# Decoder front end: first query piece, high parts and first query rows in another order

## Chip, cores and metric

The kernel runs on one core of a Trainium2 chip. The metric is the device time of one execution in microseconds (us), lower is better; where several runs are shown, their median counts.

## What is computed

A two layer decoder on x of shape (4, 256, 128) with a context of shape (4, 1601, 64). The change touches only the start: the end of the first sub-layer and the beginning of the second.

```
x = layernorm(x + L0_attn(x))             # distance attention, one head; all before about 38 us
x = layernorm(x + L0_xattn(x, ctx_512))   # 16 heads of 8
    # q, k, v   = heads(x @ Wq + bq), heads(x @ Wk + bk), heads(x @ Wv + bv)     "qs", "ks", values of x
    # qc        = heads(x @ Wcq + bcq)                                           "qc"
    # kc, vc    = heads(ctx @ Wck + bck), heads(ctx @ Wcv + bcv)                 "kc", values of the context
    # y = softmax(causal(q k^T / sqrt(8))) v + softmax(qc kc^T / sqrt(8)) vc ;  y @ Wp + bp
x = layernorm(x + L0_ffn(x))              # mixture of 8 experts, top 2
x = layernorm(x + L1_attn(x))             # gated complex recurrence
x = layernorm(x + L1_xattn(x, ctx, ctx))
x = layernorm(x + L1_ffn(x))
```

## The kernel before

**Split numbers.** The scores of the second sub-layer must be exact to float32 while the matmuls are bf16. So every projected query and key is split into three bf16 parts, high, middle and low, and a score is a matmul over 48 rows (6 products of parts by 8 channels of a head). The split is done in 22 pieces of at most 512 columns, numbered j. Pieces 0 to 3 are the context keys of batch 0 (piece 3 has 65 columns); 4, 5 and 6 are the qc, qs and ks projections of the first half of x (batches 0 and 1); 7, 8 and 9 the same of the second half; 10 to 21 are the context keys of the batches 1 to 3.

**One piece** passes through four engines. keys(j) on TensorE (PE, L592 for context, L595 for x) projects into one of two PSUM banks, j % 2. high(j) on ScalarE (ACT, L927 or L929) writes the bf16 high part. rest(j) on VectorE (DVE, L1054 or L1056) writes what is left over into rem, two buffers, j % 2. middle(j) on ACT (L934) rounds rem to the middle part. low_part(j) subtracts once more, on DVE for the pieces 4 to 6 (L1061), on GpSimd (POOL, L445) for all others.

The waits between them: keys(j) waits for rest(j-2), since that frees its bank. rest(j) waits for high(j), for middle(j-2) and for the low part of j-2, since these free its half of rem. middle(j) waits for rest(j). A piece of x waits, besides, for its half of the first layernorm's output (x_ready, L155).

**The layernorm** works per half c (512 columns): pe_ln(c), L129, centres by a matmul; act_ln(c), L139, squares; pe_ln2(c), L134, gives the variance; act_ln2(c), L144 and L150, takes its logarithm and exponential; dve_ln(c), L155, writes X.

**values(n)** projects values on PE (L612 context, L607 x) in blocks into two further PSUM banks, waiting for the copy of block n-2. The blocks 0 to 4 are context values of batch 0 and copied by DVE at L1074; 5 to 8 are values of x, two matmuls each, and copied with a bias at L1068.

**Order of work.** All engines run fixed lists in program order; nothing is rescheduled. Each list is written out by hand in one function per engine, and an engine stops at the first wait that isn't met. The lists for the pieces 4 to 9 are what the change edits, on PE, ACT and DVE.

**SyncE's queue (SP)** carries the parts to DRAM scratch and back, since a head's rows have to be brought together. split_out(kind, b), L361, writes the 6 part rows of one kind of one batch (three that are high parts of a query, then after a wait two middle, then after a wait one low). load_split(kind, m), L381, waits for all 6 at the first unit of a batch and reads them for unit m (4 heads) in two DMAs. load_context, L348, reads the context keys of a unit in two DMAs. An issue takes SP 0.4 to 0.6 us, whatever its transfer takes later. The semaphore slot_in of unit 0 counts the two context and two qc loads: the first score matmul needs those four and no others.

**The second sub-layer** then has 16 units (4 batches by 4 groups of heads) of 15 "halves". A half (half(h), L730) is two score matmuls of 128x512 whose maximum DVE takes (L1133). 22 halves run before the main loop; in that ramp the pieces 10 to 21 and the other context values are interleaved, one after nearly each half. The first half needs slot_in of unit 0, values(8) ahead of it on PE, and nothing else that is late. The main loop (from `for g in range(NU * NST)`) has 240 steps: scores again, transposed (L772), exponentials on ACT (L1009), outputs (L795), and one more half. Its first step waits for the row of maxima of unit 0, brought by four small DMAs (L389).

The lists that matter, PE, ACT and DVE:

```
PE : ... keys(3) pe_ln(1) values(0) pe_ln2(1) keys(4) keys(5) values(1) keys(6) values(2) ...
ACT: ... high(3) act_ln(1) middle(3) act_ln2(1) high(4) ; for j in 5..9: middle(j-1) high(j)
DVE: ... dve_ln(0) rest(3) values(0) dve_ln(1) rest(4) rest(5) low_part(4) values(1) rest(6) ...
```

Of the kernel before, what the change touches and what calls it, by code (L numbers as in the profile page):

```python
# [82 lines left out]
def decoder_program(nc, a, out):  # L83
    persistent = ExitStack()
    with persistent:
# [119 lines left out]
        with ExitStack() as st:  # L205
# [85 lines left out]
            def low_on_dve(j):  # L291

                return FIRST_X <= j < SECOND_X

            def lows(j):

                return (x_low if low_on_dve(j) else c_low), sum(low_on_dve(i) == low_on_dve(j) for i in range(j + 1))
# [42 lines left out]
            with nc.Block() as block:  # L340
                @block.sync
                def _(sp):
# [5 lines left out]
                            sp.dma_start(kc[s][head_rows(e)], kc_scr[b, row:row + HD].rearrange(  # L348
                                "c r j t -> (c r) (j t)")).then_inc(slot_in[s], 16)

                    def split_out(kind, b):

                        j = last_piece[groups.index((kind, b // 2))]
                        q = slice(b * TQ, (b + 1) * TQ)
                        rows = KPART if kind == "ks" else QPART
                        for part, ready in enumerate(((j_hi, j + 1), (j_mid, j + 1), lows(j))):
                            sp.wait_ge(*ready)
                            for r in range(6):
                                if rows[r] == part:
                                    src = xk[:, part, q] if kind == "ks" else xq[:, PART_AT[part], ("qc", "qs").index(kind), q]  # L360
                                    sp.dma_start(xs_scr[kind][b, :, r], src).then_inc(x_out[kind][b], 16)  # L361
# [10 lines left out]
                    def load_split(kind, m):  # L372

                        s, b, g = m % SLOTS, m // NG, m % NG
                        if g == 0:
                            sp.wait_ge(x_out[kind][b], 16 * 6)
                        for e in range(2):
                            row = 16 * g + HD * e
                            dst = ks[s][head_rows(e)] if kind == "ks" else qq[s][head_rows(e), ("qc", "qs").index(kind)]
                            src = xs_scr[kind][b, row:row + HD].rearrange("c r j t -> (c r) (j t)")  # L380
                            sp.dma_start(dst, src).then_inc(slot_in[s] if kind == "qc" else self_in[s], 16)  # L381
# [16 lines left out]
                    for j, c0, w in FIRST_SLABS:  # L398
                        for ready, part in (((j_hi, j + 1), hi), ((j_mid, j + 1), mid), (lows(j), low)):
                            sp.wait_ge(*ready)  # L400
                            for r in range(6):
                                if (hi, mid, low)[KPART[r]] is part:
                                    sp.dma_start(kc_scr[0, :, r, :, c0:c0 + w], part[:, 0, c0:c0 + w]).then_inc(first_out, 16)
                    sp.wait_ge(filled, 2 * SLOTS)
                    sp.wait_ge(*KEYS_OUT[0])
                    load_context(0)
                    split_out("qc", 0)
                    split_out("qs", 0)
                    load_split("qc", 0)
                    split_out("ks", 0)  # L410
                    load_split("qs", 0)
                    load_split("ks", 0)
# [170 lines left out]
                def _(pe):  # L583
# [13 lines left out]
                    def values(n):  # L597

                        if n >= 2:
                            wait_values_out(pe, n - 2)  # L600
                        b, t0, count = values_order[n] if values_order[n][0] != "x" else (values_order[n][1], None, 2)
                        w = H * VW
                        if t0 is not None:
                            pe.wait_ge(ld_ctx[b], 16)
                        for i in range(count):
                            if t0 is None:
                                last = pe.matmul(ps[:, 2 + n % 2, i * w:(i + 1) * w],  # L607
                                                 X[:, (2 * b + i) * 128:(2 * b + i + 1) * 128], wv_x, start=True, stop=True)
                            else:
                                t = t0 + i  # L610
                                k = 128 if t < NKT - 1 else KLAST
                                last = pe.matmul(ps[0:k, 2 + n % 2, i * w:(i + 1) * w],  # L612
                                                 ctx_t[:, b, t * 128:t * 128 + k], wcv, start=True, stop=True)
                        last.then_inc(v_ps, 1)
# [84 lines left out]
                    project(1)  # L699
                    keys(3)  # L700
                    pe_ln(1)
                    values(0)
                    pe_ln2(1)
                    keys(4)
                    keys(5)
                    values(1)
                    for i in range(3):
# [199 lines left out]
                def _(act):  # L907
# [24 lines left out]
                    def middle(j):  # L932
                        act.wait_ge(j_rem, j + 1)
                        act.activation(parts_of(j)[1], rem[:, j % 2, 0:pieces[j][2]], ACT.Copy).then_inc(j_mid, 1)  # L934
# [38 lines left out]
                    high(3)  # L973
                    act_ln(1)
                    middle(3)
                    act_ln2(1)
                    high(4)
                    for j in range(5, LATE_KEYS):
                        middle(j - 1)
                        high(j)  # L980
                    for h in range(HALVES + S1_LEAD):
                        if h == 0:
                            middle(LATE_KEYS - 1)
# [38 lines left out]
                def _(dve):  # L1022
# [84 lines left out]
                    residual(1)  # L1107
                    dve_ln(0)
                    rest(3)
                    values(0)  # L1110
                    dve_ln(1)
                    rest(4)
                    rest(5)
                    low_part(4)
                    values(1)
# [1422 lines left out]
```

## Time and profile before

| | us |
|---|---|
| median of 3 runs | 656.49 (656.16 to 658.83) |
| the profiled execution, its own time | 657.46 |
| its span from first to last instruction | 655.7 |
| PE busy | 605.3 (92%) |
| DVE busy | 518.6 (79%) |
| ACT busy | 448.8 (68%) |
| POOL busy | 217.6 (33%) |
| mean granted TensorE clock, share of full | 0.979 |

The time of an execution is its span and 1.76 us around it. A timeline row reads: start, duration, engine, line, operation, output <- inputs, count, and in brackets how long the engine had been idle and what ended that. PEld rows are weight loads beside the matmuls; SPq rows are the issue of a DMA, not its transfer.

### The profile page before, as it was taken

How to read it: one execution, taken by the hardware profiler on the slowest of the kernel's cores; microseconds unless marked ns; L12 is line 12 of the kernel's file. 1: busy time of each engine (PE TensorE's matmuls, PEld its weight loads, DVE VectorE, ACT ScalarE, POOL GpSimd, SP SyncE). 2: the span in 40 equal slices, each digit the busy share in tenths (PEclk: the TensorE clock that was granted, in tenths of full speed). 3: DMA queues.
4: the chain of work that ended last, by engine and by line, in shares of the span. 5: the costliest groups of instructions: out<-in, count | busy, mean ns of one | idle time of the engine just before them, and what ended most of it. 6: DMA issues, size and time to landing. Idle time of an engine off the chain costs nothing. (4 is left out here: it accounts for less than half of the span.)

```text
span 655.7 us, 13652 instructions
## 1 busy us (share of the span) xinstructions
PE 605.3 (92%) x5208; PEld 335.6 (51%) x5208; DVE 518.6 (79%) x710; ACT 448.8 (68%) x818; POOL 217.6 (33%) x296
## 2 busy tenths in 40 slices
PE   9989999999999999999999899999728799999995
PEld 5644544444444444444433468777214466567884
DVE  5369999999999999999963469889599468786532
ACT  3555589999999999999998445556681256666214
POOL 8214443335666576667665003010000000024000
PEclk9999999999999999999999979999959999999999
DMA  8357586566666444434320217893000100000000
GB/s 212 108 142 224 199 258 179 155 171 173 174 170 165 132 105 92 99 86 115 72 64 22 74 52 232 304 333 135 1 0 1 48 1 0 2 1 0 1 0 33
DMA packets 44895, 71.11 MB, mean 108 GB/s; under 512 B 13048, under 2 KB 32544, under 8 KB 44832
## 3 DMA queue, kind: packets, MB, share of 16 engines
q1 hardware_dynamic: 31840, 38.34, 22.3%
q0 software_dynamic: 12384, 29.66, 13.8%
q10 hardware_dynamic: 608, 2.25, 1.5%
q8 instruction: 41, 0.67, 0.4%
q14 instruction: 22, 0.18, 0.1%
HBM read 44.68 MB, written 24.80 MB: 106 GB/s over the span
## 5 line engine op out<-in xcount | busy, mean ns | idle before, releaser
L1009 ACT ACTIVATE prob<-ps 128x512 f32<-128x512 f32 (+2 forms) x480 | 250.9, 584 | 23.5 <-PE ps L772 15.4
L1133 DVE TENSOR_REDUCE pm<-ps 128x2 f32<-128x1024 f32 x192 | 224.1, 1209 | 5.7 <-PE ps L730 5.6
L795 PE MATMUL ps<-prob,vst 128*9 128x256 f32 (+1 forms) x1664 | 131.7, 381 | 3.2 <-ACT o_all L997 3.2
L772 PE MATMUL ps<-qq,kc 50*128 50x256 bf16 (+1 forms) x832 | 132.2, 273 | 0.6 <-DMA qq<-mrow 0.6
L730 PE MATMUL ps<-kc,qq 48*128 48x512 bf16 x384 | 117.3, 383 | 1.3 <-DVE pm L1133 1.2
L772 PEld LDWEIGHTS ps<-qq,kc 50*128 50x128 bf16 (+1 forms) x832 | 52.2, 95 | 96.2 <-ACT prob L1009 79.1
L795 PEld LDWEIGHTS ps<-prob,vst 128*9 128x9 f32 (+1 forms) x1664 | 27.7, 88 | 44.5 <-ACT prob L1009 28.2
L718 PE MATMUL ps<-masks_b 64*128 64x256 bf16 x256 | 38.0, 269 | 0.0
L730 PEld LDWEIGHTS ps<-kc,qq 48*128 48x128 bf16 x384 | 33.9, 93 | 6.9 <-DVE pm L1133 3.4
L1466 ACT ACTIVATE sg<-ps,exp_bias 128x512 f32<-128x512 f32 x32 | 22.0, 686 | 21.8 <-PE ps L1382 21.8
L535 POOL TENSOR_TENSOR o_all<-o_all,below 128x512 f32<-128x512 f32 x14 | 17.8, 1270 | 50.6 <-DMA below<-rden_scr 50.6
L1140 DVE TENSOR_REDUCE nm<-ps 128x4 f32<-128x512 f32 (+1 forms) x32 | 30.6, 957 | 2.0 <-PE ps L718 0.8
L1380 PE MATMUL ps<-x_high,up_high 128*128 128x512 f32 x64 | 26.7, 417 | 5.3 <-DMA exp_bias<-in_wexp 3.7
L545 POOL DMA_DIRECT2D R<-o_all x56 | 28.9, 522 | 4.1 <-POOL o_all L537 4.1
L2133 ACT ACTIVATE ctx_t<-ps,base 128x512 f32<-128x512 f32 x16 | 11.0, 688 | 27.8 <-PE ps L1863 27.8
L2075 ACT ACTIVATE ps<-shift 128x512 f32<-128x512 f32 (+1 forms) x28 | 15.7, 569 | 20.2 <-DVE shift L2328 14.1
L1566 DVE SCALAR_TENSOR_TENSOR hv<-ps,exp_bias,sg 128x512 f32<-128x512 f32 x32 | 24.0, 750 | 4.3 <-ACT sg L1466 4.2
L1471 ACT ACTIVATE hh_high<-whole 128x512 fp32r<-128x512 f32 x32 | 20.0, 626 | 10.4 <-DVE whole L1574 10.1
L1744 POOL TENSOR_TENSOR ctx<-ctx_t,ctx 128x512 fp32r<-128x512 f32 x4 | 5.2, 1290 | 65.5 <-DVE ctx L2340 65.5
L1382 PE MATMUL ps<-x_high,up_low 128*128 128x512 f32 x64 | 26.3, 411 | 0.0
L1381 PE MATMUL ps<-x_low,up_high 128*128 128x512 f32 x64 | 26.1, 408 | 0.0
L445 POOL TENSOR_TENSOR low<-rem,mid 128x512 bf16<-128x512 f32 (+1 forms) x16 | 14.6, 920 | 33.8 <-ACT mid L934 33.8
(369 smaller groups left out, 1262.6 us busy)
## 6 DMA issues: line engine op xcount, KB each, us to landing
kc<-kc_scr SPq DMA_DIRECT2D x32, 300.2 KB, 4.6
below<-rden_scr POOLq DMA_DIRECT2D x14, 256.0 KB, 6.0
comb_bc<-comb_scr SPq DMA_DIRECT2D x7, 512.0 KB, 6.1
ctx<-ctx_scr POOLq DMA_DIRECT2D x4, 801.0 KB, 7.0
raw<-in_wexp POOLq DMA_DIRECT2D x8, 384.0 KB, 6.4
exp_scr<-raw_high POOLq DMA_DIRECT2D x8, 384.0 KB, 4.7
exp_scr<-raw_low POOLq DMA_DIRECT2D x8, 384.0 KB, 6.0
kc_scr<-hi SPq DMA_DIRECT2D x6, 400.2 KB, 4.8
```

The source lines that it names most:

```text
L545: pool.dma_start(R[row:row + HD, b * TQ:(b + 1) * TQ], o_all[32 * hh:32 * hh + HD, n, 0:TQ]).then_inc(y_in[b], 16)
L718: done = pe.matmul(o, ident_b[rows, half, :], mask[rows, half, :].unsqueeze(1).to_broadcast([64, 2, 128]), start=False, stop=(half == 1), ...
L730: return pe.matmul(bank, qq[s][rows, 0, j, t * 128:(t + 1) * 128], kc[s][rows, j, c * 512:(c + 1) * 512], start=True, stop=True)
L772: last = pe.matmul(bank[0:p, j * TQ:(j + 1) * TQ], kc[s][rows, j, t * 128:t * 128 + p], qq[s][rows, 0, j, :], start=(j == 0), stop=True, s ...
L795: last = pe.matmul(o_ps[32 * hh:32 * hh + VW, kind * TQ + q0:(kind + 1) * TQ], value[:, hh * VW:(hh + 1) * VW], prob[0:k, (NST * n + t) % ...
L1009: act.activation(prob[0:p, g % P_RING, 2 * e:2 * e + 2, q0:TQ], s2[0:p, k % S2_RING, 0:2 * w].rearrange("p (i q) -> p i q", i=2), ACT.Exp, ...
L1133: dve.tensor_reduce(pm[:, m % 2, c, :, jt], banks, AX.X, ALU.max).then_inc(s1_read, 1)
L1140: dve.tensor_reduce(nm[:, :, 1, :].rearrange("p e (j t) -> p e j t", t=2)[:, :, :, t], banks[:, :, 0:2 * w].rearrange("p e (j n) -> p e j ...
L1380: pe.matmul(o, weight[0], x[0], start=start, stop=False, skip_group_check=True)
L1381: pe.matmul(o, weight[0], x[1], start=False, stop=False, skip_group_check=True)
L1382: return pe.matmul(o, weight[1], x[0], start=False, stop=True, skip_group_check=True)
L1566: dve.scalar_tensor_tensor(out=hv[:, k % 2, :], in0=ps[:, 2 + k % 2, :], scalar=exp_bias[s][:, NF + f:NF + f + 1], in1=sg[:, k % 2, :], op ...
```

## The change

Four edits, all in the lists of the front:

1. PE: keys(4) goes ahead of pe_ln2(1), and values(0) behind it.
2. ACT: high(4) goes ahead of act_ln2(1); and for the pieces 5 to 9, high(j) goes ahead of middle(j-1).
3. DVE: rest(4) goes ahead of values(0) and dve_ln(1).
4. SP: the six qc rows of batch 0 are written ahead of the context load of unit 0; and the qc load of unit 0 goes ahead of the middle and low rows of qs.

No operation is added or taken away. The compiled lists have the same operations, waits and shapes; the line numbers of the new kernel are one higher from L356 on.

```diff
@@ sync
-                    def split_out(kind, b):
+                    def split_out(kind, b, parts=range(3)):
...
-                        for part, ready in enumerate(((j_hi, j + 1), (j_mid, j + 1), lows(j))):
+                        for part, ready in [(i, ((j_hi, j + 1), (j_mid, j + 1), lows(j))[i]) for i in parts]:
...
                     sp.wait_ge(filled, 2 * SLOTS)
+                    split_out("qc", 0)
                     sp.wait_ge(*KEYS_OUT[0])
                     load_context(0)
-                    split_out("qc", 0)
-                    split_out("qs", 0)
+                    split_out("qs", 0, (0,))
                     load_split("qc", 0)
+                    split_out("qs", 0, (1, 2))
                     split_out("ks", 0)
@@ tensor
                     pe_ln(1)
+                    keys(4)
+                    pe_ln2(1)
                     values(0)
-                    pe_ln2(1)
-                    keys(4)
                     keys(5)
@@ scalar
                     middle(3)
+                    high(4)
                     act_ln2(1)
-                    high(4)
                     for j in range(5, LATE_KEYS):
+                        high(j)
                         middle(j - 1)
-                        high(j)
@@ vector
                     rest(3)
+                    rest(4)
                     values(0)
                     dve_ln(1)
-                    rest(4)
                     rest(5)
```

How the compiled lists move. TensorE from the projection of piece 3 to that of piece 5; L134 is the variance of the second half, L595 a piece of x, L612 the context values. Before:

```order
L592 MATMUL ps<-ctx_t,proj_w 128x65 [waits ld_ctx0,j_rem]
L129 MATMUL ps<-R,base 128x512 [waits g_r]
L612 MATMUL ps<-proj_w,ctx_t 128x144 [waits ld_ctx0]
L612 MATMUL ps<-proj_w,ctx_t 128x144 x2
L134 MATMUL ps<-qsq,base 128x512 [waits ln1_squared]
L595 MATMUL ps<-X,proj_w 128x512 [waits ln1_x,j_rem] x2
```

and now:

```order
L593 MATMUL ps<-ctx_t,proj_w 128x65 [waits ld_ctx0,j_rem]
L129 MATMUL ps<-R,base 128x512 [waits g_r]
L596 MATMUL ps<-X,proj_w 128x512 [waits ln1_x,j_rem]
L134 MATMUL ps<-qsq,base 128x512 [waits ln1_squared]
L613 MATMUL ps<-proj_w,ctx_t 128x144 [waits ld_ctx0]
L613 MATMUL ps<-proj_w,ctx_t 128x144 x2
L596 MATMUL ps<-X,proj_w 128x512 [waits ln1_x,j_rem]
```

Piece 4 now stands between the centring and the variance of the second half, and the values block comes after both.

ScalarE from the second half's squares to the middle part of piece 6; L929 is a high part, L934 a middle part, L144 and L150 the layernorm. Before:

```order
L139 ACTIVATE qsq<-ps 128x512 [waits ln1_centred]
L934 ACTIVATE mid<-rem 128x65 [waits j_rem]
L144 ACTIVATE ln_ln<-ps,base 128x512 [waits ln1_var]
L150 ACTIVATE ln_rstd<-ln_ln 128x512 [waits ln1_lnv]
L929 ACTIVATE xq<-ps,base 128x512 [waits j_ps]
L934 ACTIVATE xq<-rem 128x512 [waits j_rem]
L929 ACTIVATE xq<-ps,base 128x512 [waits j_ps]
L934 ACTIVATE xq<-rem 128x512 [waits j_rem]
L929 ACTIVATE xk<-ps,base 128x512 [waits j_ps]
L934 ACTIVATE xk<-rem 128x512 [waits j_rem]
```

and now:

```order
L139 ACTIVATE qsq<-ps 128x512 [waits ln1_centred]
L935 ACTIVATE mid<-rem 128x65 [waits j_rem]
L930 ACTIVATE xq<-ps,base 128x512 [waits j_ps]
L144 ACTIVATE ln_ln<-ps,base 128x512 [waits ln1_var]
L150 ACTIVATE ln_rstd<-ln_ln 128x512 [waits ln1_lnv]
L930 ACTIVATE xq<-ps,base 128x512 [waits j_ps]
L935 ACTIVATE xq<-rem 128x512 [waits j_rem]
L930 ACTIVATE xk<-ps,base 128x512 [waits j_ps]
L935 ACTIVATE xq<-rem 128x512 [waits j_rem]
```

The high part of a piece now comes before the middle part of the piece ahead of it, and that of piece 4 before the layernorm's last two steps.

SyncE's queue from the last context slab to the rows of ks, as one piece of the difference:

```order
 L403 DMA kc_scr<-low 64x2x577 [waits c_low]
-L348 DMA kc<-kc_scr 48x3202 [waits first_out,filled]
-L348 DMA kc<-kc_scr 48x3202
-L361 DMA qc_scr<-xq 64x2x256 [waits j_hi]
+L361 DMA qc_scr<-xq 64x2x256 [waits j_hi,filled]
 L361 DMA qc_scr<-xq 64x2x256 x2
 L361 DMA qc_scr<-xq 64x2x256 [waits j_mid]
 L361 DMA qc_scr<-xq 64x2x256
 L361 DMA qc_scr<-xq 64x2x256 [waits x_low]
-L361 DMA qs_scr<-xq 64x2x256 [waits j_hi]
-L361 DMA qs_scr<-xq 64x2x256 x2
+L348 DMA kc<-kc_scr 48x3202 [waits first_out]
+L348 DMA kc<-kc_scr 48x3202
+L361 DMA qs_scr<-xq 64x2x256 [waits j_hi]
+L361 DMA qs_scr<-xq 64x2x256 x2
+L381 DMA qq<-qc_scr 48x512 [waits qc_out0]
+L381 DMA qq<-qc_scr 48x512
 L361 DMA qs_scr<-xq 64x2x256 [waits j_mid]
 L361 DMA qs_scr<-xq 64x2x256
 L361 DMA qs_scr<-xq 64x2x256 [waits x_low]
-L381 DMA qq<-qc_scr 48x512 [waits qc_out0]
-L381 DMA qq<-qc_scr 48x512
```

The context load moved behind six writes, and the qc load ahead of three.

## Rows read from the trace of the kernel before

**Rows 1.** Busy time by stretch: engine busy us (instructions), PEclk, DMA share, GB/s
```profile
33.00:51.00 18.00, 14.61 (x60) 8.43 (x60) 11.28 (x21) 9.56 (x18) 3.88 (x5) 1.00 0.52 140
51.00:83.00 32.00, 30.14 (x177) 16.54 (x176) 29.99 (x38) 18.34 (x40) 14.21 (x19) 1.00 0.68 216
83.00:150.00 67.00, 66.35 (x903) 27.96 (x899) 64.73 (x72) 61.84 (x118) 25.54 (x36) 1.00 0.65 185
```

**Rows 2.** Timeline, the ramp's last reductions and the main loop's first matmul
```profile
78.09 12.52 DVE L1133 TENSOR_REDUCE pm<-ps 128x2 f32<-128x1024 f32 x11
...
82.58 0.27 PE L772 MATMUL ps<-qq,kc 50*128 50x256 bf16 x1 [0.58 <-DMA qq<-mrow]
```

**Rows 3.** Timeline, 33 to 51 us, the rows of the pieces 4 to 9
```profile
33.17 0.69 DVE L155 TENSOR_TENSOR X<-ps,ln_rstd 128x512 f32<-128x512 f32 x1 [0.20 <-ACT ln_rstd L150]
...
33.98 0.90 PE L612 MATMUL ps<-proj_w,ctx_t 128*128 128x144 f32 x6
...
34.83 1.13 PE L134 MATMUL ps<-qsq,base 128*128 128x512 f32 x2
...
36.00 0.69 ACT L144 ACTIVATE ln_ln<-ps,base 128x512 f32<-128x512 f32 x1 [1.07 <-PE ps L134]
...
36.42 0.60 SPq L403 DMA_DIRECT2D kc_scr<-low  x1
...
36.72 0.63 ACT L150 ACTIVATE ln_rstd<-ln_ln 128x512 f32<-128x512 f32 x1
...
37.25 0.67 ACT L929 ACTIVATE xq<-ps,base 128x512 bf16<-128x512 f32 x1
37.38 0.69 DVE L155 TENSOR_TENSOR X<-ps,ln_rstd 128x512 f32<-128x512 f32 x1 [1.85 <-ACT ln_rstd L150]
...
38.78 1.12 PE L595 MATMUL ps<-X,proj_w 128*128 128x512 f32 x2 [0.37 <-DVE rem L1056]
...
39.17 0.82 SPq L348 DMA_DIRECT2D kc<-kc_scr  x2
...
40.00 0.75 DVE L1056 SCALAR_TENSOR_TENSOR rem<-ps,base,xq 128x512 f32<-128x512 f32 x1 [1.27 <-ACT xq L929]
40.04 3.76 SPq L361 DMA_DIRECT2D qc_scr<-xq  x6
40.67 0.68 DVE L1061 TENSOR_TENSOR xq<-rem,xq 128x512 bf16<-128x512 f32 x1
40.78 0.63 ACT L934 ACTIVATE xq<-rem 128x512 bf16<-128x512 f32 x1 [0.82 <-DVE rem L1056]
...
41.32 0.67 ACT L929 ACTIVATE xk<-ps,base 128x512 bf16<-128x512 f32 x1
...
42.02 0.75 DVE L1056 SCALAR_TENSOR_TENSOR rem<-ps,base,xk 128x512 f32<-128x512 f32 x1 [0.16 <-ACT xk L929]
...
45.89 1.16 POOL L445 TENSOR_TENSOR xq<-rem,xq 128x512 bf16<-128x512 f32 x1 [10.57 <-ACT xq L934]
...
47.71 1.06 SPq L381 DMA_DIRECT2D qq<-qc_scr  x2
...
48.45 0.75 DVE L1056 SCALAR_TENSOR_TENSOR rem<-ps,base,xk 128x512 f32<-128x512 f32 x1 [1.06 <-ACT xk L929]
...
50.80 0.39 PE L730 MATMUL ps<-kc,qq 48*128 48x512 bf16 x2
```

**Rows 4.** Landing times of the DMAs of qq, of L361 and of L348
```profile
DMA to landing us min/median/max: 1.9/2.9/4.8
...
DMA to landing us min/median/max: 1.9/2.0/4.3
...
DMA to landing us min/median/max: 3.9/4.4/4.9
```

**Rows 5.** Busy time by stretch, columns as in rows 1, edges of a low clock
```profile
376.00:377.00 1.00, 1.00 (x3) 0.78 (x3) 0.69 (x1) 0.24 (x2) 0.00 (x0) 0.50 1.02 380
...
386.00:387.00 1.00, 1.00 (x10) 1.00 (x9) 0.10 (x1) 0.60 (x1) 0.00 (x0) 0.88 0.00 0
```

## Prediction, made before the changed kernel ran

> **What bounds the kernel now.** I read the busy times by stretch first [rows 1]. From 83 us on the main loop has TensorE busy 66.35 of 67.00 us; it is a fixed amount of work, and whatever makes it start earlier moves all behind it. In the ramp ahead of it, 51 to 83 us, VectorE has 29.99 of 32.00 and TensorE 30.14: full as well, and none of its work is changed. The loose stretch is 33 to 51 us, where TensorE has 14.61 of 18.00, VectorE 11.28 and ScalarE 9.56: a latency chain through four engines. The ramp hands over to the loop with VectorE's reductions back to back and TensorE waiting 0.58 us for the row of maxima of unit 0 [rows 2], both of which are timed by the ramp's start. So the question is how much sooner the first score matmul, now at 50.80 us, can start, and the kernel gains just that.
>
> The timeline of that stretch [rows 3] shows the cycle. rest(5) starts at 40.00, middle(5) follows at 40.78, high(6) only behind it at 41.32, rest(6) at 42.02: 2.02 us a piece, each step waiting for the one before. The bracket at 42.02 names high(6) as what VectorE waited for, the one at 48.45 names high(9), after 1.06 us idle. But high(j) doesn't depend on middle(j-1); only the list says so. The end of it: rest(9) at 48.45, four small values blocks with their copies, first score at 50.80, which is 2.35 us later.
>
> The other thing that the first score needs is the qc load of unit 0. It is issued at 47.71 over 1.06 us; such loads land after 1.9 to 4.8 us [rows 4]. With 2.0 the second, issued about 48.25, is there at 50.25: not the last wait, but within 0.55 us of it. So the three engines' edits alone could give only some 0.5 us, and SP's alone nothing; both are needed.
>
> **The sum, part by part.** Steps used, all from [rows 3]: a projection takes TensorE 1.12 us and a values block 0.90, and the next block can begin a little before the end (the variance at 34.83, 0.85 after the values block's start); I estimate 0.96 and 0.90 from start to start, and with the full 1.12 the four projections up to keys(7) would come out 0.6 later in all; what reads a projection starts 1.16 after it (the variance at 34.83 is read at 36.00); high to rest 0.70 (41.32 to 42.02); rest to middle 0.78 (40.00 to 40.78); one to the next on ScalarE 0.54 (40.78 to 41.32); middle to a low part 0.70 too; a rest holds VectorE 0.67 (40.00 to 40.67), a low part some 0.60, and I take the same for a copy.
>
> *Piece 4 ahead of the variance.* X of the first half is written at 33.17+0.69=33.86, and TensorE takes its next block at 33.98. keys(4) takes that slot instead of values(0). high(4) at 35.15 instead of 37.25, rest(4) at 35.85. The price: the variance starts at 34.94 or a little more instead of 34.83, since the squares were ready but TensorE is held 0.1 longer; the logarithm goes from 36.00 to about 36.14, dve_ln(1) from 37.38 to 37.52. I charge 0.14 us, and it falls on nobody: X of the second half is first read by keys(7), which comes at about 40.6. values(0) goes back to 35.95, copied at 36.9, ahead of dve_ln(1) on VectorE; its copy ends by 37.5, so it costs dve_ln(1) nothing more.
>
> *Pieces 5 and 6.* keys(5) stands behind values(0): 35.95+0.90=36.85. high(5) 38.00, rest(5) 38.70 (was 40.00), middle(4) 38.55, low_part(4) 39.35 (was 40.67). keys(6) follows values(1) at 38.71, high(6) 39.86, rest(6) 40.56 (was 42.02), middle(5) 40.42.
>
> *Piece 7 gives some of it back.* keys(7) follows values(2) at 40.57, high(7) 41.72. middle(6) now stands behind high(7): 42.27, and low_part(6) needs it: 42.97. VectorE's list has rest(7) behind low_part(6), so rest(7) starts at 43.57, 3.01 after rest(6). This is the cost of the swap on ScalarE: every middle part comes later against its own rest than it did. It is the narrowest point of my chain.
>
> *Pieces 8 and 9.* keys(8) at 42.43 isn't held by it, high(8) 43.58, rest(8) behind rest(7) and a copy at 44.84. keys(9) waits for rest(7), 43.57+0.78=44.35; high(9) 45.51, and rest(9) could start at 46.21. It also waits for the low part of piece 7, on POOL: middle(7) at 43.57+0.78=44.35, POOL at 45.05, 1.16 us long, 46.21. The two agree, so I take 46.25. Against 48.45 that is 2.20 us, and the first score is free to start at 46.25+2.35=48.60.
>
> *SP.* The last slab row is issued by 37.02. qc high rows: three at about 0.6, to 38.8 (6 in 3.76). Middle(4) ends 38.55+0.63=39.2: two rows to 40.4. Low_part(4) ends at 40.0: one row to 41.0. Context load 41.0 to 41.9 (39.17 before), landing by 4.9 at the latest: 46.8 or so. That is 1.8 us ahead of 48.60, so moving it later costs nothing. qs high rows to 43.7. The qc load waits for the last of the qc rows, issued about 40.4 and landing within 2.0 to 4.3: 44.7 at worst. Its two issues end between 44.8 and 45.8, against 48.77 before. What is pushed back: three qs rows by one load, and those feed the self scores, the last two of the unit's 15 halves; SP as a whole has nothing more to issue than before and starts 2 us sooner.
>
> How late does that load land? In the trace loads of qq took 1.9 to 4.8 [rows 4]. With 1.9 the second lands at about 46.7, with 4.8 at about 49.5, which would be 0.9 us after 48.60. The first is nearest to the load it replaces, alone in its stretch; but now the context load runs beside it until about 46. I take 3 us, 47.7: hidden, by 0.9. The Trainium skill ("DMA: Bandwidth & Descriptors", section "Issuing engines are not separate DMA queues") says that all transfers share the same 16 DMA engines and interleave, whoever issues them; by it alone the qc load would be slowed by the context load beside it, which speaks for the 4.8 and a gain of 1.3.
>
> **Sum:** 2.2 us, between 1.3 (load lands late, or the 0.6 of the projections and a little more) and 2.9 (each of the seven handovers behind keys(4) a tenth shorter than I took it). The profiled execution took 657.46, so by its own account 655.3; the median of the runs is 656.49, 0.97 lower, and the forecast is made against that: 654.3 us. That is 0.33%, and less than the 0.5% (3.3 us) that a measurement of this kernel can tell from no change.
>
> **Rivals.**
>
> *A, the gain is mostly lost before the first score: 655.5.* Either the load lands at its worst and rest(7) slips behind the later middle(6) by another half microsecond, or the handover at 82.58 has a price that I don't see, the four small DMAs of the maxima meeting other transfers. For it: the DMA share is already 0.68 in the ramp. Against it: SP is ahead of, not behind, its old times. Gain 0 to 1.2.
>
> *B, the clock falls once more: 659.7.* In this trace TensorE's granted clock drops from 2.4 to 1.2 GHz at 376 us, behind two short idle spells in the expert stage's start, and is back in the slice that begins at 386 [rows 5], 10.9 us in all. Everything after the front now runs 2.2 us sooner against whatever times that decision. Should such a fall come on another thin place on TensorE's path, it costs at most half its length, 5.4 us, and the sum is 656.49-2.2+5.4=659.7, slower than before by 0.49%; a longer one would pass 0.5%. It decides at a TensorE busy share that is near what made it fall at 376. Against it: work and gaps behind the front are the same. The Trainium skill ("TensorE: Matmul & The Clock Gate", Part 1) says that the monitor's phase isn't tied to a kernel's start, so that the same kernel can vary from run to run; by that rule the shift changes nothing in the median, which already samples it.
>
> *C, the fall at 376 doesn't come: 648.9.* The same mechanism the other way: at most half of the 10.9 us would be saved, 5.4: 656.49-2.2-5.4=648.9 at the lowest.
>
> *D, the change doesn't do what it says:* keys(4) not taking the slot at 33.98, because X's semaphore comes after TensorE has gone to wait elsewhere. TensorE's list has nothing in between, so it would just wait; it costs 0.1 to 0.2 us and the variance behind it as much. It is inside my range.
>
> **How the numbers follow.** Forecast with its bounds 0.76; A 0.13; B 0.05, of which 0.03 beyond 0.5%; C 0.04; left over 0.02. Faster by over 0.5% (below 653.2) needs C, or the upper end of the forecast with a lucky median: 0.04+0.04=0.08. Slower by over 0.5% (above 659.8): 0.03. Same: 0.89. The range goes from the upper bound of the gain, 656.49-2.9=653.6, widened to 652.9 for the spread of medians, to 656.6, which takes in A and a median as high as before's own.
>
> **What would show it.** The first score matmul (L731 there) at 48.6, within 0.6; rest(4) at about 35.9; rest(7) at 43.6, with VectorE having waited for ScalarE's middle part ahead of it; dve_ln(1) at 37.5; SP's qc load at 44 to 45; the first matmul of the main loop at 80.4; each later stage shifted by the same 2.2. I am wrong if the first score names the DMA of qq as what it waited for, if it starts at 48.6 but the loop doesn't start at 80.4, or if the stages behind 83 us have other lengths than before.

## The result, and the profile after

| | us |
|---|---|
| the change, median of 6 runs | 652.53 (651.38 to 653.23) |
| before, median of 6 runs | 657.14 (656.16 to 658.83) |
| ratio | 0.9938, 95% interval 0.9916 to 0.9959 |
| the change's profiled execution, its span | 652.77, 651.0 |

The change is faster by 0.6%, 4.1 us by the ratio. All 19 executions of the change in this study have a median of 652.5, all 104 of the kernel before one of 656.4: 3.9 us (3.2 to 4.5 by resampling them). I forecast 2.2. Single executions of either kernel lie over 4 to 9 us, so below every difference is read twice: as a time, and as a place in the profile.

The busy times by stretch of the change, which answer to [rows 1]:

```profile
31.00:49.00 18.00, 15.44 (x67) 9.20 (x66) 13.32 (x24) 11.46 (x20) 4.90 (x5) 1.00 0.55 140
49.00:81.00 32.00, 30.06 (x180) 16.62 (x181) 29.95 (x38) 19.14 (x42) 15.10 (x20) 1.00 0.71 225
81.00:148.00 67.00, 66.35 (x906) 28.16 (x902) 64.72 (x72) 61.76 (x119) 25.60 (x35) 1.00 0.63 181
```

Ramp and main loop are what they were (66.35 of 67.00 us on TensorE in both); only the stretch ahead is fuller. Its timeline answers to [rows 2] and [rows 3]; columns as there, line numbers one higher:

```profile
33.12 0.69 DVE L155 TENSOR_TENSOR X<-ps,ln_rstd 128x512 f32<-128x512 f32 x1 [0.20 <-ACT ln_rstd L150]
...
33.95 1.10 PE L596 MATMUL ps<-X,proj_w 128*128 128x512 f32 x2
...
34.89 1.02 PE L134 MATMUL ps<-qsq,base 128*128 128x512 f32 x2
...
35.75 0.90 PE L613 MATMUL ps<-proj_w,ctx_t 128*128 128x144 f32 x6
35.81 0.75 DVE L1057 SCALAR_TENSOR_TENSOR rem<-ps,base,xq 128x512 f32<-128x512 f32 x1 [1.87 <-ACT xq L930]
...
36.48 1.02 PE L596 MATMUL ps<-X,proj_w 128*128 128x512 f32 x2
...
37.33 0.69 DVE L155 TENSOR_TENSOR X<-ps,ln_rstd 128x512 f32<-128x512 f32 x1
37.34 0.90 PE L613 MATMUL ps<-proj_w,ctx_t 128*128 128x144 f32 x6
...
38.08 1.02 PE L596 MATMUL ps<-X,proj_w 128*128 128x512 f32 x2
...
39.67 1.02 PE L596 MATMUL ps<-X,proj_w 128*128 128x512 f32 x2
...
41.30 0.60 DVE L1075 COPY vst<-ps 128x432 f32<-128x432 f32 x1
41.31 0.62 ACT L935 ACTIVATE xk<-rem 128x512 bf16<-128x512 f32 x1
41.97 0.69 DVE L1062 TENSOR_TENSOR xk<-rem,xk 128x512 bf16<-128x512 f32 x1
...
42.57 0.75 DVE L1057 SCALAR_TENSOR_TENSOR rem<-ps,base,xq 128x512 f32<-128x512 f32 x1
...
43.84 1.06 SPq L381 DMA_DIRECT2D qq<-qc_scr  x2
44.06 1.17 POOL L446 TENSOR_TENSOR xq<-rem,xq 128x512 bf16<-128x512 f32 x1 [8.79 <-ACT xq L935]
...
45.36 0.75 DVE L1057 SCALAR_TENSOR_TENSOR rem<-ps,base,xk 128x512 f32<-128x512 f32 x1 [0.66 <-POOL xq L446]
...
46.53 1.25 PE L608 MATMUL ps<-proj_w,X 128*128 128x144 f32 x8 [1.01 <-DVE vss L1069]
...
47.80 0.39 PE L731 MATMUL ps<-kc,qq 48*128 48x512 bf16 x2
```

The first score is at 47.80 instead of 50.80, and 2.95 us of it are the change's, since the row at 33.12 ahead of it had come 0.05 sooner. The cycle is broken: the projections of the pieces 5, 6 and 7 start at 36.48, 38.08 and 39.67, 1.59 us apart. Before, those of the pieces 6 and 7 waited for a rest, at 38.78 [rows 3] and 2.03 us later:

```profile
40.81 1.12 PE L595 MATMUL ps<-X,proj_w 128*128 128x512 f32 x2 [0.16 <-DVE rem L1056]
```

The main loop's first matmul shows that all of it arrives:

```profile
79.67 0.27 PE L773 MATMUL ps<-qq,kc 50*128 50x256 bf16 x1 [0.66 <-DMA qq<-mrow]
```

79.67 against 82.58 is 2.91. The two profiled executions differ by 4.7 us of span, though. The other 1.7 come in the expert stage, where the clock differs:

```profile
371.00:372.00 1.00, 1.00 (x2) 0.00 (x0) 0.00 (x0) 0.00 (x0) 0.00 (x0) 0.58 0.94 272
...
374.00:375.00 1.00, 1.00 (x4) 0.77 (x4) 0.42 (x1) 0.55 (x1) 0.00 (x0) 0.72 0.96 310
...
378.00:379.00 1.00, 1.00 (x4) 0.81 (x3) 0.97 (x12) 0.99 (x2) 0.00 (x0) 0.50 0.00 0
...
381.00:382.00 1.00, 1.00 (x9) 1.00 (x9) 0.75 (x1) 0.06 (x1) 0.00 (x0) 0.80 0.00 0
```

In this execution TensorE ran at 1.2 GHz from 371 to 375 and from 378 to 382, 6.8 us in all; in that of before for 10.2 at one stretch (the clock column of [rows 5] has it at half from 376 to 386 and for the first quarter of the slice behind; the prediction has 10.9). Whether that belongs to the change was the question for the experiments.

### The profile page after: what moved, and what is told of

Read it like the earlier page. It is cut to its first block and busy times, and to the rows that moved or that the text cites. A ratio compares the mean times of both kernels' runs of the same rounds, so it can differ in the third digit from the quotient of the medians.

```text
span 651.0 us, 13652 instructions
## 1 busy us (share of the span) xinstructions
PE 602.3 (93%) x5208; PEld 333.6 (51%) x5208; DVE 518.1 (80%) x710; ACT 448.9 (69%) x818; POOL 216.9 (33%) x296
## 5 line engine op out<-in xcount | busy, mean ns | idle before, releaser
L796 PEld LDWEIGHTS ps<-prob,vst 128*9 128x9 f32 (+1 forms) x1664 | 27.7, 88 | 44.5 <-ACT prob L1010 28.2
```

The lines of the kernel that those rows point to most:

```text
L796: last = pe.matmul(o_ps[32 * hh:32 * hh + VW, kind * TQ + q0:(kind + 1) * TQ], value[:, hh * VW:(hh + 1) * VW], prob[0:k, (NST * n + t) % ...
```

## Experiments

Every row of this table is one profiled execution. X is the start of the first half's layernorm product (L155), which no edit touches; the next two columns are the distances from it to the first score and to the main loop's first matmul. "Clock" says whether the granted clock fell to half at 49 to 54 us, and "expert stage" is the time from the layernorm matmul at its start to the last of its residual sums. "Median" and number of executions belong to that kernel's own runs.

| kernel | X to first score | X to loop | clock | expert stage | median (n) |
|---|---|---|---|---|---|
| before | 17.63 | 49.41 | no fall | 88.59 | 656.4 (104, all) |
| before_again | 17.90 | 51.04 | falls | 85.57 | |
| before_look3 | 17.83 | 50.95 | falls | 86.89 | |
| before_look4 | 17.64 | 49.41 | no fall | 88.43 | |
| the change | 14.68 | 46.55 | no fall | 86.90 | 652.5 (19, all) |
| after_again | 14.64 | 46.49 | no fall | 85.87 | |
| after_look3 | 14.58 | 46.44 | no fall | 86.49 | |
| e1_sp_old | 16.79 | 50.01 | falls | 86.57 | 657.7 (12) |
| e2_sp_only | 18.29 | 51.26 | falls | 88.15 | 656.0 (12) |
| e3_no_piece4 | 15.64 | 47.79 | no fall | 88.05 | 654.1 (12) |
| e4_no_swap | 16.11 | 48.30 | no fall | 85.80 | 655.0 (12) |
| e5_rest7_first | 14.77 | 46.63 | no fall | 86.03 | 652.3 (12) |
| e6_before_filled | 17.63 | 49.58 | no fall | 88.00 | 655.4 (12) |
| e7_load_first | 14.12 | 46.12 | no fall | 85.24 | 652.3 (9) |

**e1_sp_old: the engines' edits without SP's.**

```diff
+                    sp.wait_ge(*KEYS_OUT[0])
+                    load_context(0)
                     split_out("qc", 0)
-                    sp.wait_ge(*KEYS_OUT[0])
-                    load_context(0)
-                    split_out("qs", 0, (0,))
+                    split_out("qs", 0)
                     load_split("qc", 0)
-                    split_out("qs", 0, (1, 2))
```

> The change with SP's list as it was before; the other three engines' lists as changed. My theory: the first score needs both the engines' edits and SP's. With the old list the context load goes at about 39.2, six qc and six qs writes follow without a gap, the qc load of unit 0 is issued at about 47.3 and lands about 2 us after its second half, so the first score matmul waits for the DMA of qq and starts at 49.6 to 50.0 (50.80 before, 47.80 in the change); the time is 0.8 to 1.2 us below before. Rival (the queue's order is worth nothing, since the load was hidden): first score at 47.8, gain as in the change.

```profile
47.20 1.06 SPq L381 DMA_DIRECT2D qq<-qc_scr  x2
...
49.87 0.39 PE L730 MATMUL ps<-kc,qq 48*128 48x512 bf16 x2 [2.15 <-issue]
50.20 2.08 PE L592 MATMUL ps<-ctx_t,proj_w 128*128 128x512 f32 x2
...
53.55 1.22 DVE L1133 TENSOR_REDUCE pm<-ps 128x2 f32<-128x1024 f32 x1
```

The place was right: load at 47.20, first score at 49.87, TensorE idle for 2.15 us ahead of it. ("issue" means that the profile shows no releaser; the second load went out at about 47.8 and the two landed after 1.9 to 2.1, so it is the load.) The time was wrong: 657.7, ratio 1.0029 (1.0006 to 1.0053), so slower than before and not 0.8 to 1.2 us faster. Behind the idle spell the clock fell:

```profile
50.00:51.00 1.00, 1.00 (x3) 0.50 (x2) 0.70 (x1) 0.00 (x0) 0.00 (x0) 0.60 0.43 119
```

The projection behind the score then takes 2.08 us instead of 1.13 (50.20), and the second reduction begins 3.25 us after the first (50.30 to 53.55); in the kernel before these are 2.24 apart. From first score to loop it took 33.22 us against 31.78 in the kernel before, 1.4 us given back, so the loop starts 0.6 later than in the executions of the kernel before without a fall. That doesn't explain the whole median: over its 12 executions the mean clock was 0.9781, against 0.9829 for the kernel before beside it, and one fall as at 50 us (3.4 us at half clock in 655) lowers it by 0.0026. So in others there were further or longer falls; where, no profile here shows. At equal mean clock (by the line in the last section) e1 is 1.0 us below before, 0.4 to 1.5 with 95%: the 0.8 to 1.2 that I had expected of the order, and the clock took more than that back.

**e2_sp_only: SP's list alone**, PE, ACT and DVE as before.

> Only SP's list as changed; the other engines as before. My theory: the qc load is issued at about 46.3 or sooner, but TensorE reaches the first score at 50.8 as before: within 0.2 us of before up to the end of the main loop (first loop matmul at 82.6). Rival (the load was the last wait before): first score up to 0.5 us sooner. For the second question, where 1.7 us beyond the front came from: if they hang on the shift of the later stages, this kernel shows none of it; if they vary from run to run, it may show some.

Load issued at 44.7, and the first score no sooner: 18.29 from X against 17.63, later by 0.66, in an execution whose clock fell just before 50 us: the values block ahead of the score took 1.91 us instead of 1.25. 656.0, ratio 1.0000 (0.9975 to 1.0025). No gain of SP's part alone is seen. With e1, which brings the first score 0.8 sooner, this settles that neither part gives the 3 us without the other.

**e3_no_piece4: the swap and SP's list, piece 4 where it was.**

```diff
-                    keys(4)
-                    pe_ln2(1)
                     values(0)
+                    pe_ln2(1)
+                    keys(4)
...
-                    high(4)
                     act_ln2(1)
+                    high(4)
...
-                    rest(4)
                     values(0)
                     dve_ln(1)
+                    rest(4)
```

> The change without piece 4 ahead of the second half's variance (PE, ACT and DVE lists of that place as before); the swap of high and middle for the pieces 5 to 9 and SP's list kept. My theory: the swap breaks the 2.0 us cycle by itself, and piece 4 early gives a head start that only partly lasts: high(4) at 37.3, first score at about 48.5, 0.7 later than in the change. Rival (piece 4 is the whole gain, the swap nothing): first score at 50.5 or later.

First score 15.64 from X: 2.0 sooner than before and 1.0 later than the change, where I had 0.7. Of the 1.0 TensorE waited the last 0.23 us, by the same reading as in e1 for the qc load, which went out at 44.7 here. Ratio 0.9963 (0.9942 to 0.9984).

**e4_no_swap: piece 4 early and SP's list, middle(j-1) ahead of high(j) as before.**

```diff
                     for j in range(5, LATE_KEYS):
-                        high(j)
                         middle(j - 1)
+                        high(j)
```

> The change without the swap of high(j) and middle(j-1) for the pieces 5 to 9; piece 4 early and SP's list kept. My theory: the old cycle of about 2.02 us a piece comes back, from rest(5) at about 38.6 instead of 40.00, so the first score is at about 49.4, 1.4 before the old kernel's and 1.6 after the change's. Rival (the swap only moves the wait to the later middle parts and gives nothing): first score at 47.8.

First score at 16.11 from X: 1.5 sooner than before, 1.5 later than the change. The cycle is back in its rows, 2.03 us from rest to rest, with the same waits as before:

```profile
38.38 0.75 DVE L1057 SCALAR_TENSOR_TENSOR rem<-ps,base,xq 128x512 f32<-128x512 f32 x1 [0.41 <-ACT xq L930]
...
39.17 0.63 ACT L935 ACTIVATE xq<-rem 128x512 bf16<-128x512 f32 x1 [0.82 <-DVE rem L1057]
39.71 0.67 ACT L930 ACTIVATE xk<-ps,base 128x512 bf16<-128x512 f32 x1
40.41 0.75 DVE L1057 SCALAR_TENSOR_TENSOR rem<-ps,base,xk 128x512 f32<-128x512 f32 x1 [0.16 <-ACT xk L930]
```

The time, 655.0 with a ratio of 0.9986 (0.9963 to 1.0008), is smaller in its gain than 1.5 us but its interval holds that. So of the 3.0 us at the first score piece 4 gives 1.0 on top of the swap and 1.5 without it, the swap 1.5 on top of piece 4 and 2.0 without it. At the loop's start e3 and e4 are only 1.6 and 1.1 sooner than before: 0.4 us of their gain are lost in the ramp, which happens to neither kernel of the first pair; why, no run here shows.

**before_again, after_again, before_look3, before_look4 and after_look3** are the two kernels unchanged.

> The kernel before, unchanged, for a second profile and for the mean granted clock of many runs beside the change's. Theory 1 (what the change gains beyond the 3.0 us of the first score comes from the clock, which falls in some executions at TensorE's idle spell ahead of the first score): some of its executions have the fall at about 50 us; its mean clock over the runs is below that of the change by 0.001 to 0.002. Theory 2 (the excess of the first comparison was luck in few runs): equal mean clock.

> The change, unchanged, in more runs. Theory 1: 4 to 4.6 us below before, of which 3.0 at equal clock (5.4 us of time go with 0.01 of mean clock in the runs so far) and the rest by a higher mean clock; no fall at 46 to 54 us in its profile. Theory 2: 3.0 us below before at the same mean clock.

> The kernel before once more, for its profile alone: does the clock fall at about 50 us? So far it did in one profile of two of this kernel, and in one of one with TensorE's list of before and SP's changed. Theory (the idle spells at 46 to 50 us leave it near the fall): in some profiles; where it falls, the first score starts at 51.0 or later after the same upstream times, and the main loop about 1.3 us later than where it doesn't.

> As the run above: a fourth profile of the kernel before. Fall at about 50 us or not, loop start at about 83.9 or 82.5.

> The change once more, for its profile alone. Theory: no fall at 46 to 54 us, as in both profiles so far, first score at 47.5 to 47.8, loop start at 79.4 to 79.7. Rival (the change has the same fall in other executions): a fall there and a loop start above 80.5.

Two places were missed in them: before_look3 has the fall and its first score at 50.77, not 51.0 or later, and the last profile of the change starts it at 47.39, below 47.5 (both had X earlier, at 32.94 and 32.81).

The kernel before runs in two ways at 50 us. The rows of before_again, with the fall:

```profile
50.00:51.00 1.00, 1.00 (x9) 0.72 (x7) 0.46 (x1) 0.00 (x0) 0.99 (x1) 0.67 0.31 88
52.00:53.00 1.00, 1.00 (x2) 0.01 (x1) 0.85 (x1) 0.00 (x0) 0.00 (x0) 0.50 0.38 106
53.00:54.00 1.00, 1.00 (x4) 0.17 (x3) 0.00 (x0) 0.38 (x1) 0.00 (x0) 0.62 0.32 84
```

and in before_look4, without:

```profile
50.00:51.00 1.00, 1.00 (x8) 0.63 (x7) 0.88 (x3) 0.00 (x0) 0.78 (x1) 1.00 0.43 120
51.00:52.00 1.00, 1.00 (x4) 0.19 (x3) 1.00 (x2) 0.04 (x1) 0.00 (x0) 1.00 0.28 76
```

What goes before it is TensorE's two spells of idling, which end at 47.34 and 49.51:

```profile
47.34 0.76 PE L607 MATMUL ps<-proj_w,X 128*128 128x144 f32 x4 [0.62 <-DVE vst L1074]
...
49.51 1.53 PE L607 MATMUL ps<-proj_w,X 128*128 128x144 f32 x8 [1.42 <-DVE vss L1068]
```

But before_look4, without a fall, has the same two:

```profile
47.12 0.76 PE L607 MATMUL ps<-proj_w,X 128*128 128x144 f32 x4 [0.62 <-DVE vst L1074]
...
49.30 1.25 PE L607 MATMUL ps<-proj_w,X 128*128 128x144 f32 x8 [1.42 <-DVE vss L1068]
```

The loop is 1.5 to 1.6 us later in the executions with the fall (50.95 and 51.04 from X, against 49.41 twice). It came in two of four profiles of the kernel before and in e2, which has the same TensorE list; e4 has the same two spells and no fall. It came in none of three of the change, whose last idle spell is 1.01 us. So the spells of 0.62 and 1.42 us were followed by a fall in three of six profiles; 0 of 3 against that can be chance, and that the spells cause it is argued, not shown.

A sum by this account would be 3.0 us of list order, and in about half of the executions 1.5 more, 3.7 on the mean; measured were 3.9 between the medians of all runs. The record doesn't bear the second term out. after_again gave 652.6 with a ratio of 0.9959 (0.9933 to 0.9985), and a mean clock over 12 runs of 0.9820, below the 0.9829 of before_again, against theory 1. Over all runs the mean clock of both kernels is the same to 0.001, and at equal mean clock the change is still 3.7 us below before (3.2 to 4.1 with 95%), not 3.0. And what the fall costs at the loop's start isn't seen in whole executions: the two profiled ones of the kernel before with the fall took 655.76 and 656.92 us, the two without it 657.46 and 658.68, and the clock was low for less time in the former (23.3 and 24.4 us in all, against 26.3 and 25.0). So 3.0 us are shown by place, and some 0.7 more were measured whose source is open. e3 shows how far such sums can be off: at equal mean clock it is 2.9 us below before, with a loop start only 1.6 sooner.

**The expert stage** varies in one and the same kernel: 85.57 to 88.59 in the executions of the kernel before, 85.87 to 86.90 in those of the change, 85.24 to 88.15 in the others, whose code there is the same. It goes with its own low clock: without any it took 85.2 to 86.0 us (e4, e5, e7), with 10.2 us of it 88.1 to 88.6 (before, e2, e3). The 1.7 us of the first pair of profiles are within that spread. Whether the earlier start shifts the odds there, three profiles against four can't tell. The table's loop distances are what the list order is shown to be worth.

**e6_before_filled: the kernel before with the idle spell filled.**

```diff
                     for i in range(4):
+                        if i == 2:
+                            pe.wait_ge(masks_cast, 1)
+                            still = masks_b[:].rearrange("p i h n -> p (i h n)")
+                            for _ in range(6):
+                                pe.matmul(ps[:, 7, :], still[:, 0:128], still[:, 0:512], start=True, stop=True)
                         values(5 + i)
```

> The kernel before with six matmuls of 128x512 (results unused) on TensorE between values(6) and values(7), where it otherwise waits 1.4 us ahead of the first score; nothing else moves. Theory 1: the first score stays at 50.8 (within 0.2), the fall of the clock at about 50 us goes away, the mean clock over the runs rises by 0.001 or more and the median falls by 0.5 to 1 us. Theory 2 (no such fall, or it costs nothing, since VectorE bounds the ramp): time and clock as before.

```profile
47.83 1.46 PE L716 MATMUL ps<-masks_b 128*128 128x512 bf16 x6
49.41 1.25 PE L607 MATMUL ps<-proj_w,X 128*128 128x144 f32 x8
50.59 0.39 PE L735 MATMUL ps<-kc,qq 48*128 48x512 bf16 x2
```

First score where it was (17.63), no fall in its one profile, which half of the profiles of the kernel before don't have either. 655.4 against 656.2 for the kernel before beside it, mean clock 0.9836 against 0.9827: the way of theory 1, but the ratio is 0.9996 (0.9970 to 1.0022), so inconclusive.

**e5_rest7_first: a better order on VectorE.**

```diff
                     values(2)
+                    rest(7)
                     low_part(6)
-                    for i in range(2):
-                        rest(7 + i)
-                        values(3 + i)
+                    rest(8)
+                    values(3)
+                    values(4)
                     rest(9)
```

> The change, and on DVE rest(7) ahead of low_part(6), rest(8) ahead of the copy values(3). It aims at the place where the swap on ScalarE cost something: in the change's profile rest(7) starts at 42.57 behind a low part that waited for the later middle(6), while high(7) is ready for it at 41.4. Theory: rest(7) at 41.9, keys(9) 0.7 sooner, middle(7) and POOL's low part of piece 7 0.6 to 0.7 sooner, rest(9) at 44.7, first score at 47.1 (47.80 in the change), the time 0.7 below the change's. Rival (POOL's low parts or ScalarE are the bound at that point): first score within 0.2 of 47.8.

```profile
41.65 0.74 DVE L1057 SCALAR_TENSOR_TENSOR rem<-ps,base,xq 128x512 f32<-128x512 f32 x1
...
43.67 1.05 SPq L381 DMA_DIRECT2D qq<-qc_scr  x2
...
44.71 0.75 DVE L1057 SCALAR_TENSOR_TENSOR rem<-ps,base,xk 128x512 f32<-128x512 f32 x1
...
45.88 1.25 PE L608 MATMUL ps<-proj_w,X 128*128 128x144 f32 x8 [0.20 <-DVE vss L1069]
...
47.71 0.39 PE L731 MATMUL ps<-kc,qq 48*128 48x512 bf16 x2 [0.58 <-issue]
```

rest(7) at 41.65 and rest(9) at 44.71 came as forecast (0.18 of that from an earlier X), and TensorE was done with its values at 47.13. It then idled 0.58 us: the qc load, second half out at about 44.3, takes 3.3 to 3.5 us beside the context load, so it lands at 47.6 or a little later. The 0.5 us won on the engines, counted from X, were lost at the load, a limit that I had not seen right behind the one removed. So the first score and the time were missed (47.71 and 652.3, not 47.1 and 0.7 below the change's 652.5); the place is the rival's, by another cause than the rival's.

**e7_load_first: the same, and the qc load ahead of all qs rows.**

```diff
-                    split_out("qs", 0, (0,))
                     load_split("qc", 0)
-                    split_out("qs", 0, (1, 2))
+                    split_out("qs", 0)
```

> The run with rest(7) first, and on SP the qc load of unit 0 ahead of all qs rows. In the run with rest(7) first the engines were ready sooner, but the first score waited for the qc load, issued at 43.67 and landed 3.3 us after its second half. Theory: the load goes out as soon as the qc rows have landed, at about 42.5, lands by 46.5, and the first score starts when TensorE reaches it, at 47.1; loop start at about 79.0; 0.6 us below the change. Rival (the load moves but lands late beside the context load, 4 us and more): first score at 47.5 or later.

```profile
41.08 1.05 SPq L348 DMA_DIRECT2D kc<-kc_scr  x2
42.41 0.77 SPq L381 DMA_DIRECT2D qq<-qc_scr  x2
43.22 3.76 SPq L361 DMA_DIRECT2D qs_scr<-xq  x6
...
46.25 1.25 PE L607 MATMUL ps<-proj_w,X 128*128 128x144 f32 x8 [0.20 <-DVE vss L1068]
...
47.43 0.39 PE L730 MATMUL ps<-kc,qq 48*128 48x512 bf16 x2
```

The load went out 1.3 us sooner, 0.3 us behind the context load's issue, and took 4.3 to 4.5 instead of 3.3 to 3.5: the rival's landing time, but the wait is gone. The first score came at 47.43, not 47.1, since X was 0.4 late here (33.31). From X the first score comes 0.5 and the loop 0.4 sooner than in the change. Its median, 652.3 (9 runs, ratio to before 0.9936, 0.9909 to 0.9963), can't be told from the change's 652.5: it is the best of these lists by place, and its gain is not shown as a time.

## Why the prediction was right, and where it wasn't

**Direction and mechanism: right.** The gain is the shift of the first score, it needs SP's and the engines' edits together (e1, e2), and it goes through ramp and main loop undiminished: 2.95 at the first score, 2.86 at the loop's start counted from X (2.91 on the clock of the span), and from there to the expert stage 289.2 us in both profiles of the first pair (289.26 and 289.22). dve_ln(1) came at 37.33 (I had 37.52), so piece 4 ahead of the variance cost nothing. Rivals A and D are out: the gain was not lost, and keys(4) took its slot at 33.95. One of my signs of being wrong came true by the letter, the expert stage had another length (86.90 instead of 88.59); since it varies as much in the kernel before alone, it doesn't count against the mechanism.

**The first term was too small: 3.0, not 2.2.** The step that failed is the start to start distances on TensorE, "0.96 and 0.90", a term of the sum with the wrong size. The rows show 0.86 to 0.94 from a projection or the variance to the next block (34.89 to 35.75, 36.48 to 37.34), and 0.73 to 0.74 from a values block to the next (35.75 to 36.48). A piece costs 1.59 us, not 1.86. keys(7) came at 39.67, where I had 40.57, 0.9 sooner. I had guessed an overlap for the one and taken the duration for the other. The old trace had both to read: two projections in a row from 35.80 and a values block behind them at 37.51, 0.86 each, and 0.85 from the values block at 33.98 to the variance at 34.83.

**The narrowest point was not where I had it.** rest(7) came at 42.57 instead of 43.57. I had VectorE wait half a microsecond for middle(6), as the price of the swap on ScalarE, and made it a sign that it would. In the rows above the copy of a values block holds VectorE until 41.90 and middle(6) is done at 41.93; low_part(6) starts at 41.97, so the later middle part cost less than 0.1 us. What held rest(7) was VectorE's own list, which has low_part(6) ahead of it, 0.60 us, while high(7) was done at 41.42.

**What bounds the end was right in kind.** I had rest(9) held by POOL's low part and high(9) within 0.05 us. They were level: POOL's ended at 44.06 + 1.17 = 45.23, and so did high(9); VectorE's bracket at 45.36 names POOL. The handover from rest(9) to the first score was 2.44 against my 2.35. e5, with rest(7) ahead of low_part(6), got 0.5 us of engine time, which confirms that place in VectorE's list as a bound.

**The load:** I took 3 us of landing, it took 3.2 to 3.4, inside what the trace allowed. Hidden by 0.9 us in my account, it was so by some 0.1 (second half out at 44.5, first score at 47.80): that TensorE and the load came level is luck. With the engines' edits alone I had some 0.5 us; e1's first score came 0.8 sooner. The rule of the Trainium skill that I had weighed against this ("DMA: Bandwidth & Descriptors", "Issuing engines are not separate DMA queues") agrees with the rows: 1.9 to 2.0 us in the kernel before, where the context load had landed, 3.2 to 3.4 beside the end of that load, 4.3 to 4.5 in e7, right behind its issue. It cost the change nothing that can be seen, and e5 all it had won.

**The rest of the gain, some 0.7 us, is open.** I treated the clock as a rival behind the front only, with falls at 376 or later. The kernel before can have one at 50 us, and my own profile happened to be one of those without it. That the change makes it rarer would be rival B's mechanism with the other sign, but neither the mean clock nor the whole times show it (above). Rivals B and C took 10.9 us for the fall at 376 where the rows have 10.2, so their bounds were 659.4 and 649.2. C's condition came true in e4 and e7, no fall in that stage, and the stage was then some 3 us shorter than in the profile of before, not 5. As the text held, the stage's fall varies from run to run: 85.57 to 88.59 us in four profiles of the kernel before. With this agrees the rule of the Trainium skill ("TensorE: Matmul & The Clock Gate", Part 1) that the phase isn't tied to a kernel's start.

**Numbers.** 652.53 lies 0.4 us under the lower end of my range, 652.9, and "faster by over 0.5%", to which I gave 0.08, is the likelier reading of a ratio of 0.9938, though its interval, 0.9916 to 0.9959, holds both. I had drawn the lower end from a sum whose first term was 0.8 us too small.

## What to carry to other kernels

In a latency chain across in-order engines, look for an instruction that waits only because the list puts it behind another's result; moving it ahead breaks the cycle, and then look at once for the transfer that the same instruction needs, since it landed within some 0.1 us of the engines here. An engine that is brought sooner to a wait for a DMA gains little: in e1 TensorE came 3 us sooner, idled for 2.15, ran at half clock after it, and the kernel was 0.3% slower. And where the clock falls in some executions, compare distances between rows that the change touches in several profiles, and executions at equal mean clock, not the spans of two.

## What the runs showed of the hardware that I had not expected

- Two idle spells of TensorE of 0.62 and 1.42 us, with 0.76 us of matmuls between them, were followed by a fall from 2.4 to 1.2 GHz in two of four executions of one unchanged kernel, and in three of the six profiles here that have both; one of 1.01 us, in the change, by none in three. A wait of 2.15 us was followed by one in the only profile taken (e1).
- The clock was low for about 3.4 us there, and the loop came 1.5 us later although VectorE is as full as TensorE in the ramp (29.99 and 30.14 of 32.00 us): the projection behind the first score took 2.07 us instead of 1.13. The whole executions with the fall were not longer than those without it.
- Over 198 timed executions of all these kernels a straight line, with one offset for each kernel, has the time go with the mean granted clock at 5.3 us per 0.01, and what is left scatters by 0.9 us, against 1.9 without the clock: about three quarters of the variance within a kernel go with TensorE's mean clock.
